# Transformer layer on one core: loads of the first batch reordered, V of two batches made first, quantisation begun one batch later, first stack loaded in halves

## What is computed

```python
q, k, v = (einsum('btc,hcd->bhtd', x, W) + b for W, b in (Wq,bq), (Wk,bk), (Wv,bv))
probs   = softmax(einsum('bhtd,bhsd->bhts', q, k) / 4 + causal, axis=-1)
y       = (probs @ v).transpose(0, 2, 1, 3).reshape(8, 512, 256)
x       = layernorm(x + y @ Wo + bo)
wq      = lambda w: w.astype(float8_e4m3fn).astype(float32)
fuse    = silu(x @ wq(gate_w) * gate_scale) * (x @ wq(up_w) * up_scale)
x       = layernorm(x + fuse @ wq(down_w) * down_scale)
```

## Time and profile before

| | before |
|---|---|
| median of 3 runs | 570.0 us (569.93 to 570.35) |
| the profiled execution, its own time | 571.63 us |
| span in its profile | 569.9 us |
| PE busy | 536.9 us, 94% of the span |
| VectorE (DVE) busy | 455.2 us, 80% |
| ScalarE (ACT) busy | 317.7 us, 56% |
| GpSimd (POOL) busy | 229.6 us, 40% |
| mean granted clock of TensorE | 0.979 |

### The profile page before, as it was taken

How to read it: one execution, slowest core, us unless ns; L and a number is a source line. 1 busy time by engine, 2 the same in 40 slices (tenths; PEclk the granted TensorE clock), 3 DMA queues, 4 the chain that set the end, 5 groups by cost and what they waited for, 6 DMA issues and landing times.

```text
span 569.9 us, 10675 instructions
## 1 busy us (share of the span) xinstructions
PE 536.9 (94%) x3919; PEld 356.7 (63%) x3921; DVE 455.2 (80%) x808; ACT 317.7 (56%) x579; POOL 229.6 (40%) x251
## 2 busy tenths in 40 slices
PE   8787899999999999999999999997899999999992
PEld 4444365565656656556565665553478888888892
DVE  6887388788888789788888889877647889898875
ACT  3146467676576665766667666663844544445440
POOL 5015143334533534344444353332335544455542
PEclk9899799999999999999999999997999999999997
DMA  4967565746546477545754554600000011110012
GB/s 154 268 168 273 142 185 154 199 165 173 162 150 156 151 209 198 169 119 170 185 161 152 122 187 133 158 15 2 2 0 1 2 38 38 37 39 8 30 38 74
DMA packets 61516, 68.19 MB, mean 120 GB/s; under 512 B 6296, under 2 KB 55832, under 8 KB 61464
## 3 DMA queue, kind: packets, MB, share of 16 engines
q1 hardware_dynamic: 60632, 66.59, 40.4%
q10 hardware_dynamic: 832, 0.92, 0.5%
HBM read 37.62 MB, written 29.61 MB: 118 GB/s over the span
## 4 chain that ended last, share of the span: by engine, by line
PE 83%; DMA 5%; DVE 3%; issue 3%; SPq 2%; ACT 2%; POOL 1%; POOLq 0%; DVEq 0%; ACTq 0%
PE ps L1098 16%; PE ps L961 12%; PE ps L953 12%; PE ps L859 9%; PE ps L867 9%; PE ps L1107 7%; PE ps L934 7%; PE ps L935 4%; PE ps L897 2%; DMA m_scratch<-mrow 2%; PE ps L908 1%; PE ps L979 1%; PE ps L990 1%; DVE nmax L613 1%; DMA q_st<-zero_rows 1%
## 5 line engine op out<-in xcount | busy, mean ns | idle before, releaser
L613 DVE TENSOR_REDUCE nmax<-ps 128x2 f32<-128x1024 f32 (+1 forms) x192 | 197.0, 1041 | 62.4 <-PE ps L935 62.1
L446 ACT ACTIVATE probs<-ps 128x512 f32<-128x512 f32 x320 | 183.9, 596 | 82.7 <-PE ps L953 81.6
L370 POOL TENSOR_SCALAR_AFFINE_SELECT probs<-probs 128x512 f32<-128x512 f32 x128 | 90.7, 722 | 217.8 <-ACT probs L446 217.8
L953 PE MATMUL ps<-q_st,k_st 98*128 98x384 bf16 (+3 forms) x512 | 123.3, 304 | 8.1 <-DMA q_st<-m_scratch 4.5
L397 POOL TENSOR_TENSOR f_l<-f_full,f_h 128x512 fp32r<-128x512 f32 x48 | 63.5, 1324 | 73.6 <-ACT f_h L529 73.6
L934 PE MATMUL ps<-k_st,q_st 98*128 98x256 bf16 (+2 forms) x384 | 82.3, 275 | 5.4 <-DMA k_st<-k_scratch 3.2
L935 PE MATMUL ps<-k_st,q_st 124*128 124x128 bf16 x512 | 84.2, 221 | 0.0
L961 PE MATMUL ps<-probs,v_st 128*32 128x512 f32 (+3 forms) x1024 | 83.5, 444 | 0.2
L953 PEld LDWEIGHTS ps<-q_st,k_st 98*128 98x128 bf16 x512 | 44.3, 98 | 51.5 <-issue 26.0
L524 ACT ACTIVATE sgate<-ps,s_gate 128x512 f32<-128x512 f32 x48 | 32.8, 685 | 60.0 <-PE ps L1098 60.0
L935 PEld LDWEIGHTS ps<-k_st,q_st 124*128 124x128 bf16 x512 | 46.1, 98 | 19.2 <-DVE nmax L613 13.4
(11 more groups left out here) (96 smaller groups left out, 827.7 us busy)
## 6 DMA issues: line engine op xcount, KB each, us to landing
q_st<-q_scratch SPq DMA_DIRECT2D x32, 384.0 KB
k_st<-k_scratch SPq DMA_DIRECT2D x32, 384.0 KB
q_scratch<-part SPq DMA_DIRECT2D x16, 384.0 KB, 3.7
k_scratch<-part SPq DMA_DIRECT2D x16, 384.0 KB, 2.8
xT<-in_attn_xT SPq DMA_DIRECT2D x8, 512.0 KB, 3.8
q_scratch<-part SPq DMA_DIRECT2D x16, 256.0 KB, 3.9
resid<-in_attn_x SPq DMA_DIRECT2D x8, 512.0 KB, 3.8
k_scratch<-part SPq DMA_DIRECT2D x15, 256.0 KB, 2.1
```

The lines of the kernel that those rows point to most:

```text
L370: pool.affine_select(out=blocks, in_=blocks, compare_op=ALU.is_ge, fill=0.0, base=0, pattern=[*pattern, [1, P]], channel_multiplier=-1).th ...
L446: act.activation(probs[:, u, :], ps[:, u % 2, :], ACT.Exp, scale=SCALE).then_inc(exp_done, 1)
L613: dve.tensor_reduce(nmax[:, i, heads[0]:heads[-1] + 1], src, AX.X, ALU.max, negate=True).then_inc(max_taken, 1)
L953: m = pe.matmul(ps[:, u % 2, c0:c0 + T - P * j], k_st[0:RP, g, h, P * j:P * j + P], q_st[0:RP, g, h, P * j:T], start=True, stop=True)
```

## The change

- **SP, start:** xT of batch 1 is loaded before the parts of batch 0 are stored, no longer behind the first stacks. The stack of group 0 comes in two halves of two heads each, with semaphores of their own (`half_loaded`).
- **SP, batch 0:** between the round trips of groups 1 and 2 only w_o and b_o are loaded. x of batch 0 follows the stacks of batch 1 (g = 0 and 1), x of batch n+1 comes at the end of batch n behind `load_stack(n + 1, 2)`, and the raw weights follow there, one matrix at the end of each of batches 0, 1, 2 (before: batches 0, 1, 3). The scales are loaded at the end of batch 1 under a semaphore of their own.
- **V:** V of batches 0 and 1 is made at the start (batch 1 into banks 0 and 1); `work` in g = 3 and the `empty_v` there are left out for n = 0. `keep_warm` is 8 long in place of 12 and writes the bank MB.
- **VectorE:** the constant columns of `v_st` are filled before the parts are formed. Quantisation starts with w = 4, three steps in each group, and has nine steps in each of w = 30 and 31.
- **PE, end:** the feed-forward part starts after 64 steps of quantisation; the first `down` waits for all 96.
- **GpSimd:** `add_bias(n)` stands in g = 3 in place of g = 1.

```diff
-    NLATE = 5
+    NLATE, NSCALE = 2, 3
...
+        def stack_count(n, g):
+
+            return 48 * (n + 1) - (16 if g else 48)
...
                 for g in (2 * (k // 2), 2 * (k // 2) + 1):
-                    wait(sp, stack_loaded[g], n * 48 - 16)
+                    wait(sp, stack_loaded[g], stack_count(n - 1, g))
+                    if n and g == 0:
+                        for v in range(2):
+                            sp.wait_ge(half_loaded[v], 32)
...
+            load_xT(1)
             store_parts(0, 0)
...
             sp.wait_ge(mask_filled, 3)
-            load_stack(0, 0)
+
+            for k in range(2):
+                sp.wait_ge(part_stored[k], 48)
+            for v in range(2):
+                rows, heads = slice(32 * v, 32 * v + 32), slice(2 * v, 2 * v + 2)
+                sp.dma_start(q_st[RM:RP, 0, heads], q_scratch[rows].rearrange("(h d) a t -> (d a) h t", d=D)).then_inc(half_loaded[v], 16)
+                sp.dma_start(k_st[RM:RP, 0, heads], k_scratch[rows].rearrange("(h d) a t -> (d a) h t", d=D)).then_inc(half_loaded[v], 16)
             load_stack(0, 1)
-            load_xT(1)
...
                     sp.dma_start(w_o[:], wo.rearrange("(k p) n -> p k n", p=P)).then_inc(late_in, 16)
-                    for dst, src in ((b_o, bo), (s_down, down_s)):
-                        sp.dma_start(dst[:], src.partition_broadcast(P)).then_inc(late_in, 16)
-                    for dst, src in ((s_gate, gate_s), (s_up, up_s)):
-                        sp.dma_start(dst[:], src).then_inc(late_in, 16)
-                    load_x(0)
-                    load_raw(0)
+                    sp.dma_start(b_o[:], bo.partition_broadcast(P)).then_inc(late_in, 16)
                 if nxt:
-                    load_x(n + 1)
                     store_parts(n + 1, 0)
...
-                if n in (1, 3):
-                    load_raw((n + 1) // 2)
+                if n == 0:
+                    load_x(0)
                 store_mrow(n, 3)
...
                     load_stack(n + 1, 2)
+                    load_x(n + 1)
+                if n < 3:
+                    load_raw(n)
+                if n == 1:
+                    sp.dma_start(s_down[:], down_s.partition_broadcast(P)).then_inc(scales_in, 16)
+                    for dst, src in ((s_gate, gate_s), (s_up, up_s)):
+                        sp.dma_start(dst[:], src).then_inc(scales_in, 16)
...
-                    if g == 1:
+                    if g == 3:
                         add_bias(n)
...
             def first_step(w):
 
-                return 3 * (w - 2) + 3 * max(w + 2 - W, 0)
+                return 3 * (w - G) + 6 * max(w + 2 - W, 0)
...
             empty_v(0, 1, MB)
+            for v in range(2):
+                empty_v(1, v, v)
...
-                    if w > 1:
+                    if n:
                         quantize(first_step(w))
...
-                    if g == 3 and n + 1 < B:
+                    if g == 3 and 0 < n < B - 1:
                         empty_v(n + 1, 0)
...
-                        for q in range(3):
+                        for q in range(6):
                             quantize(first_step(w) + 3 + q)
...
             def first_rows():
 
                 pe.wait_ge(mpart_ready, 1)
+                pe.wait_ge(v_out, 4)
...
-                    pe.wait_ge(stack_loaded[g], (w // G + 1) * 48 - 16)
+                    if w:
+                        wait(pe, stack_loaded[g], stack_count(w // G, g))
+                if w == 0 and u in (0, 2):
+                    pe.wait_ge(half_loaded[u // 2], 32)
...
-            keep_warm(12)
+            for v in range(2):
+                project_v(1, v, None, v)
+            pe.wait_ge(v_out, 2)
+            keep_warm(8)
...
-            pe.wait_ge(quant, 8 * NQ)
+            pe.wait_ge(quant, 8 * NQ * 2 // 3)
...
                 wait(pe, down_out, n * 2)
+                if n == 0:
+                    pe.wait_ge(quant, 8 * NQ)
```

25 lines of the change are left out of this document (14 added, 11 removed).

## The result

| | before | after |
|---|---|---|
| median (9 runs each, same chip) | 570.85 us (569.36 to 571.98) | **565.2 us** (564.55 to 569.48) |
| the profiled execution, its own time | 571.63 us | 564.83 us |
| span in its profile | 569.9 us | 563.1 us |

The ratio is 0.9923, 95% interval 0.9897 to 0.9949. That is 4.4 us by the ratio and 5.65 by the medians. The nine times of the changed kernel fall in two groups, six from 564.55 to 565.57 with a mean granted clock of 0.984 to 0.986, and three from 568.92 to 569.48 with 0.978; the median shows the first group alone.

What follows compares the result with a forecast made beforehand. PE, busy 536.9 of 569.9 us, was taken as the bound, with its idle and half-clocked stretches in the first 60 us to shorten. Terms summing to -8.75 took the 570.0 us median to 561.2 us, range 558.8 to 564.3.

Steps and rivals of the forecast that it cites:

- gap before w = 2: PE's 4.54 us idle before w = 2, waiting for group 2's maxima, goes wholly: -4.5 us.
- half clock behind it: After the gap before w = 2, 5.30 us at half clock do 2.65 us of work; full clock returns: -2.65 us.
- new wait for the first stack of batch 1: In w = 2, PE wants this stack slightly before it lands at 56.5 to 57: +0.4 us, ends 0 and 1.
- V out of w = 3: Batch 1's 16 V matmuls leave w = 3, which shortens to 10.2 us: -1.6 us, ends -0.8 and -3.4.
- start: Before w = 1, earlier first scores at full clock, so w = 1 starts at 44.5: -1.1 us, ends 0 and -2.
- gate weights: In w = 4, DVE's first quantisation step waits for gate_w, landing at 79.9 to 82.2: +0.5 us, ends 0 and 2.
- end: Nine quantisation steps instead of six before `hT_l` of batch 1 delay PE slightly: +0.2 us, ends -0.3 and +1.4.
- New waits at their far ends: Rival: gate_w and batch 1's first stack both come late, with some half clock: 563.3 to 564 us; chance 0.16.
- The bias addition at g = 3: Rival: GpSimd's 2.35 us addition holds up a DVE operation, passing 0.9 us to PE eight times: 568.4 us; chance 0.04.
- lock: DVE and GpSimd share a port pair, locked for a whole instruction; such a meeting costs up to 2.35 us.
- Slower: Rival: loads of x and raw weights hold up every g = 1 round trip, 3.1 us per batch: 583 us; chance 0.03.

Runs made afterwards that it cites:

- e14: Changed kernel with x of batch 1 (512 KB) issued behind gate_w instead of ahead of it: 561.41 us.
- e13: Changed kernel, loads untouched, with the three quantisation steps of w = 4 placed behind the parts of batch 2 and four of the six reductions: 562.72 us.
- e8: e6 plus eight warm matmuls ahead of the first score matmuls of group 2 in w = 0: 562.79 us.
- e9: Changed kernel with gate_w in quarters and x of batch 1 later, quantisation from w = 5, an extra step in w = 5, 9, 13, warm matmuls as in e8: 564.32 us.
- e11: Changed kernel plus eight warm matmuls ahead of the first score matmuls of group 2 in w = 0: 567.69 us.
- e12: Changed kernel with the first stack loaded whole instead of in halves: 568.21 us.
- e2: Changed kernel with no quantisation steps in w = 4 and six in w = 5, loads left in place: 563.33 us.
- e5: Changed kernel with the gate_w load split into four, each chunk of eight quantisation steps waiting for its own quarter: 563.27 us.
- e6: Changed kernel with x of batch 1 and gate_w loaded behind the maxima of group 5, quantisation from w = 6, six steps in w = 6 and 7: 565.22 us.
- e7: e6 with three quantisation steps moved from w = 30 to the end of w = 31: 564.14 us.
- e10: e9 with the four normalisations of batch 0 moved from the end of w = 29 to its start: 559.29 us.
- e1: Changed kernel with gate_w loaded earlier, right behind the load of group 3's maxima in batch 0: 566.21 us.
- e15: e14 with the edit of e10: 558.89 us.
- e4: Changed kernel keeping mainly its load order, quantisation and bias moves; V and xT of batch 1, whole first stack and 12 warm matmuls as before: 566.37 us.

## Why the prediction missed

Point by point, in the profiled executions:

| term | forecast | measured |
|---|---|---|
| gap before w = 2 | -4.5 | -4.7 (w = 1 takes 9.4 us, before 14.1) |
| half clock behind it | -2.65 | -2.15 for this term and the next together (w = 2: 11.8 us, before 14.0) |
| new wait for the first stack of batch 1 | +0.4 | in the row above; 0.31 us of idle time |
| V out of w = 3 | -1.6 | -1.9 |
| start | -1.1 | -1.2 |
| **gate weights** | **+0.5** (0 to 2) | **+4.6** |
| end | +0.2 | -1.2 in w = 30, 0.0 in w = 31 (and -0.2 in w = 5 to 28) |

The row of the first stack, at w = 2, stands here; the forecast put it at 56.5 us:

```profile
56.66 0.34 PE L958 MATMUL ps<-k_st,q_st 98*128 98x384 bf16 x1 [0.31 <-DMA q_st<-zero_rows]
```

- **The step that failed is the gate weights.** Three things in it. First, the landing: the prediction took 6.1 to 8.4 us from two loads of the kernel before and had gate_w there at 79.9 to 82.2; it was issued at 74.47 in place of 73.8, took 8.46 us and landed at 82.93, with DVE ready for it at 80.14. The bytes were there to be counted: the stack (768 KB) and x (512 KB) are issued some 2 us or less ahead of gate_w (768 KB), together 2.10 million bytes. From issue to landing the queue moved 293 GB/s, so these are 7.2 us; the other 1.3 us went to transfers behind it, as 2.48 million bytes passed in the 8.46 us. e14 takes 512 KB from in front of it, and 1.8 us go. Second, the price, which is the larger part: the wait of DVE was put at 0.5 us in the sum, with 2 as its end, and nothing was added for the clock behind PE's idle time, though the prediction had shown what a gap costs; only a rival had it. DVE waited 2.82 us, PE 2.36, and w = 4 grew by 4.6. Third, what e13 shows: a late landing costs 3.0 us less when the step that needs it stands behind the parts of batch 2, for which PE waits, and not ahead of them. The prediction named that queue and did not ask whether its order could matter more than the landing.
- **The wait for the stack of group 2** in w = 0 was nowhere in the prediction. It hides in the start term, which looks right: the first scores came 1.0 us earlier than forecast (21.12 us, clock 1.0 in 21 to 28), w = 0, from its third unit of scores on, took 10.9 us and not the 9.6 of before, and so w = 1 started at 44.40 for 44.5: the right sum of two wrong terms. From the landing of that stack to the start of w = 1 it is 7.9 us in e8, e9, e11, e12 and e14, where the clock stays at 1.0, 8.5 to 8.7 in the changed kernel, e2, e5, e6 and e7, 9.0 in e13, 9.6 in e10 and 9.9 in e1 and e15. The landing itself lies between 35.0 and 37.2 us. The order of PE before these points is nearly the same, so the term scatters by over 1 us either way. What sets this landing was not tested.
- **The end** was off by 1.4 us in the other direction, and by chance. w = 31, where the three more steps stand, takes 10.8 us before and 10.7 after. w = 30 has a gap of over 3 us before and after, ahead of all steps that were added, but the half clock behind it is longer in before. The windows of before and of after give 0.34 x 2 x 10 = 6.8 us and 3.4 us of it:

```profile
392.00:402.00 10.00, 8.02 (x50) 3.81 (x50) 5.05 (x15) 5.07 (x11) 0.63 (x1) 0.66 0.02 3
```
```profile
386.00:396.00 10.00, 7.45 (x56) 3.69 (x60) 6.17 (x18) 5.81 (x13) 1.15 (x2) 0.83 0.02 3
```

  Among the kernels that are equal there, the stretch from w = 30 to the feed-forward part is 23.5 to 23.8 us where the half clock lasts 3.4 us and 24.5 where it lasts 6.8 (e2, e5, e8, e9).
- **From the profile to the median.** The sum gave 562.9 us for the profiled execution; 564.83 came, so 1.9 us of the miss are terms: 4.1 too little for gate_w, and about 2 that came back elsewhere, mostly in w = 30. Then 1.6 us were taken off, because before's profiled execution lay above its median. The profiled execution of the changed kernel lay 0.4 *below* its median, 565.2. That makes 2.0 us, half of the miss of 4.0 us. (By the nine runs that before has now, 570.85, the correction would have been 0.8 us.) A correction of that kind, taken from one execution of another kernel, says nothing on the new kernel's own scatter, and here the change itself brought the scatter up.
- **The rivals.** "New waits at their far ends" had the mechanism and the sign of the half clock, at 563.3 to 564. With 4.6 us in place of 0.5 for gate_w the forecast becomes 565.3, close to the 565.2 measured; this closeness is luck, as the end and the correction for the median were both wrong, in opposite directions. The bias addition at g = 3 did nothing: a batch takes 46.9 us before and after. The memsets of `v_st` kept their 912 ns beside GpSimd's mask work, so no lock showed there. The Trainium skill's "SBUF — State Buffer", SBUF: two separate sides, gives the lock to a DVE operation only in a 2-port mode or with two SBUF inputs, a condition that the prediction left out. "Slower" fell too, but its mechanism, small transfers behind large ones, is real: in e1 and e13 stores of 8 KB took 4.78 and 7.33 us, against a median of 2.3. The Trainium skill's "DMA: Bandwidth & Descriptors", Queues, rings and completion order, has each DMA engine consume its descriptors in ring order, and these rows agree.

## What to carry to other kernels

When a wait is removed, list the loads whose deadline it had been hiding: PE came to w = 4 10 us sooner, and everything that DMA had to bring by then came due 10 us sooner too. Price a landing by the bytes queued ahead of it over the rate of that stretch, not by the median of the same tile elsewhere, and take the result as the least: it gives 7.2 us for the changed kernel, 5.0 for e14 and 5.0 for e5, where 8.46, 6.70 and 7.16 were measured. And if a load is near its deadline, first try the order of the two or three loads around it, and what stands behind the wait on the waiting engine, before you change its size or move it far. A gap that feeds a clock drop is to be priced with the drop, and as a range: behind the same gap of 3.2 us the half clock lasted 3.4 us in some profiles and 6.8 in others.

## What was not expected of the hardware

- 192 KB landed 7.2 us after issue (e5) where 768 KB took 8.5: in a full queue the time is mostly that of the other transfers, those issued just behind among them. An 8 KB store took 7.3 us (e13).
- Gaps of PE in w = 0 and w = 4 and the clock behind them: all from 1.62 (e4) to 3.02 us (e11) were followed by a stretch at half clock, 1.30 (e14), 1.32 and 1.37 (e12) and 1.40 us (e15, in w = 4) by none. But in e10 a gap of 0.80 us, behind eight warm matmuls, was followed by a window at 0.65, and in e8, e9 and e11 gaps of 0.99, 0.93 and 0.64 behind the same matmuls were not. The length of the gap alone does not decide it, and in w = 28 of e11, e14 and e15 the clock fell to half without a gap over 0.6 us.
- One more quantisation step of about 0.5 us in a group with three costs 0.3 to 0.5 us of the whole, though DVE is busy 81% of the span: DVE has next to no slack within these groups. Three steps fewer ahead of `hT_l` in w = 31 gave 0.6 us (e7).
